# Pair 0 of an attention kernel: two vertical taps moved between two statistics, a copy and a store moved ahead, and one tile's additions moved from TensorE to VectorE

## The reference

```python
def _L0_conv_ref(x, W_qkv, W_proj, b_proj):
    qkv = x_flat @ W_qkv.T
    q, k, v = (qkv[0], qkv[1], qkv[2])
    var_v = jnp.var(v, axis=-1, ddof=1, keepdims=True)
    var_k = jnp.var(k, axis=-1, ddof=1, keepdims=True)
    scores = var_v @ jnp.swapaxes(var_k, -2, -1) * scale
    attn = jax.nn.softmax(scores, axis=-1)
    out = attn @ v
    out = out @ W_proj.T + b_proj
...
# layer 1, offset is fixed per group of 16 channels
    kern = jnp.exp(-(kx * kx + ky * ky) / (2.0 * SIGMA * SIGMA))
    kern = kern / kern.sum(axis=(1, 2), keepdims=True)
    out = lax.conv_general_dilated(shifted, kern_c[:, None, :, :], ..., feature_group_count=C)
...
x = x + _L0_conv_ref(_gn(x), L0_conv_W_qkv, L0_conv_W_proj, L0_conv_b_proj)
x = x + _L1_conv_ref(_gn(x), L1_conv_offset)
```

## Time and profile before

| | |
|---|---|
| median of three runs | 2025.69 us |
| the profiled execution | 2027.71 us |
| its span, first to last instruction | 2026.0 us |
| DVE busy | 1739.5 us (86%) |
| ACT busy | 1206.9 us (60%) |
| POOL busy | 276.1 us (14%) |
| mean granted TensorE clock | 0.997 of 2.4 GHz |

### The profile page before, as it was taken

One profiled execution on the slowest core, in us unless ns is written; L12 is line 12 of the kernel. 1 busy time (PEld: TensorE's weight loads), 2 busy tenths in 40 slices (PEclk: granted clock), 3 DMA queues, 4 the chain that ended last, 5 costly groups with the idle time before them and its releaser, 6 DMA issues.

```text
span 2026.0 us, 33485 instructions
## 1 busy us (share of the span) xinstructions
PE 1966.9 (97%) x12672; PEld 1109.0 (55%) x12672; DVE 1739.5 (86%) x3663; ACT 1206.9 (60%) x1322; POOL 276.1 (14%) x324
## 2 busy tenths in 40 slices
PE   5999989999999999999999999999999999999997
PEld 4755437563565536654375634756356553665443
DVE  7887686998779987899869998699878998599977
ACT  3667634776367762778527783477636776277820
POOL 2100001111012110111001111111101211011121
PEclk9999999999999999999999999999999999999999
DMA  8212313545235552356424562354523554134515
GB/s 331 84 54 64 105 63 87 138 141 169 85 116 158 148 177 63 116 137 185 139 64 128 152 190 86 92 139 137 167 84 118 155 154 129 43 116 137 157 42 187
DMA packets 110193, 255.19 MB, mean 126 GB/s; under 512 B 47312, under 2 KB 48080, under 8 KB 110032
## 3 DMA queue, kind: packets, MB, share of 16 engines
q0 software_dynamic: 31968, 116.41, 19.6%
q1 hardware_dynamic: 72016, 114.62, 18.7%
q10 hardware_dynamic: 6048, 22.02, 3.3%
HBM read 172.93 MB, written 79.73 MB: 125 GB/s over the span
## 4 chain that ended last, share of the span: by engine, by line
PE 60%; DVE 22%; issue 8%; DMA 5%; ACT 4%; SPq 0%; ACTq 0%; POOL 0%; DVEq 0%; POOLq 0%
PE ps L1405 23%; PE ps L1464 17%; PE ps L1447 16%; DVE bt L940 9%; DVE st L892 4%; ACT ring L714 3%; DMA a_sb<-a_rows 2%; PE ps L1422 2%; DMA a_rows<-at 2%; DVE bt L1064 1%; DVE bt L1061 1%; DVE xv L1074 1%; DVE xv L1077 1%; DVE xv L969 1%; DMA xv<-in_L_conv_W_qkv 1%
## 5 line engine op out<-in xcount | busy, mean ns | idle before, releaser
L714 ACT ACTIVATE ring<-a_sb,coef 128x1024 f32<-128x1024 f32 x768 | 817.9, 1137 | 22.9 <-issue 10.0
L1405 PE MATMUL ps<-wkv_hi,h_sp 128*128 128x256 f16 x4608 | 771.8, 273 | 12.0 <-DVE wkv_lo L1260 10.7
L1447 PE MATMUL ps<-ring,xv 128*64 128x512 f32 x3072 | 688.3, 596 | 7.5 <-ACT ring L714 6.2
L1405 PE MATMUL ps<-wkv_lo,h_sp 128*128 128x256 f16 x2304 | 628.9, 273 | 0.0
L940 DVE TENSOR_TENSOR bt<-bt,ring 128x1024 f32<-128x1024 f32 x528 | 615.3, 1214 | 3.0 <-ACT ring L714 1.9
L1405 PEld LDWEIGHTS ps<-wkv_hi,h_sp 128*128 128x128 f16 x4608 | 451.6, 98 | 91.7 <-issue 26.8
L1447 PEld LDWEIGHTS ps<-ring,xv 128*64 128x64 f32 x3072 | 209.2, 137 | 424.7 <-issue 384.1
L698 ACT ACTIVATE xv<-ps 128x256 f32<-128x256 f32 x192 | 72.6, 382 | 522.9 <-DVE st L892 522.0
L1464 PE MATMUL ps<-xv,wp_hi 128*128 128x512 f16 x1152 | 351.4, 380 | 6.2 <-DVE xv L1184 4.5
L892 DVE BATCH_NORM_STATS2 st<-ps 128x6 f32<-128x64 f32 x1536 | 218.0, 214 | 116.1 <-PE ps L1405 115.1
L1405 PEld LDWEIGHTS ps<-wkv_lo,h_sp 128*128 128x128 f16 x2304 | 225.8, 98 | 26.7
(11 more groups left out here) (174 smaller groups left out, 1349.8 us busy)
## 6 DMA issues: line engine op xcount, KB each, us to landing
a_sb<-a_rows SPq DMA_DIRECT2D x96, 512.0 KB, 4.5
out<-xv POOLq DMA_DIRECT2D x84, 512.0 KB, 5.3
xv<-in_x POOLq DMA_DIRECT2D x48, 512.0 KB, 3.6
h_sp<-in_x ACTq DMA_DIRECT2D x42, 512.0 KB, 5.1
shift_rows<-bt POOLq DMA_DIRECT2D x42, 512.0 KB, 3.4
bt<-r_rows SPq DMA_DIRECT2D x80, 256.0 KB, 4.2
bt<-in_x SPq DMA_DIRECT2D x24, 512.0 KB, 9.3
shift_rows<-ring SPq DMA_DIRECT2D x12, 528.0 KB, 15.5
```

The source lines that it names most:

```text
L714: nc.scalar.activation(ring_of(p, s, m), a_sb[:, h % 4, :], ACT.Exp, scale=coef[:, h, m:m + 1]).then_inc(s_exp, 1)
L1405: last = nc.tensor.matmul(ps[:, kv_bank[u % 2], half * 2 * P:(half + 1) * 2 * P], h_sp[:, k, hp, m * P:(m + 1) * P], wkv[wpart][:, k, q * ...
L1447: last = nc.tensor.matmul(ps[s * HD:(s + 1) * HD, o_bank[p % 2] + j, :], v_sb[:, p, m, s * HD:(s + 1) * HD], ring_of(p, s, m)[:, j * HALF: ...
```

## The change

Four edits:

1. `MD[0]` goes from 7 to 8. In pair 0 of each of the eight images DVE adds key tile 7 as well, and PE's sum over that tile's exponentials is left out.
2. Where a layer 1 runs beside (seven images), `taps_y` of tile 0 goes from behind the additions of key tile 3 to between the statistics of unit 6 and those of unit 7.
3. `middle_tap` of tile 0 goes on ACT from behind the exponentials of key tile 3 to behind those of key tile 0.
4. The residual store of tile 0 goes on POOL from behind the first reduction of the next image (`k_reduce`) to ahead of the square root of layer 1's group statistics (`group_pow`, L444).

```diff
-        MD = (7, 8, 8, 8, 6, 8)
+        MD = (8, 8, 8, 8, 6, 8)
...
+            def store_residual(b, t):
+                pool.wait_ge(s_x1, (b + 1) * PU)
+                hold(pool, s_held_pool)
+                pool.dma_start(out_t[b, :, t, :], x1[:, t, :]).then_inc(s_res, 16)
+
             def layer1(b, with_next):
                 for t in range(CT + 1):
                     if t < CT:
                         k_reduce(b + 1, t)
-                        pool.wait_ge(s_x1, (b + 1) * PU)
-                        hold(pool, s_held_pool)
-                        pool.dma_start(out_t[b, :, t, :], x1[:, t, :]).then_inc(s_res, 16)
+                        if t:
+                            store_residual(b, t)
...
             def body(b, with_next):
+                store_residual(b, 0)
                 group_pow(pool, "y", b)
                 layer1(b, with_next)
...
                         exps(b, p, m)
                         if p and m == 2:
                             d_copy(b, p - 1, later)
+                        if later and m == (3 if p else 0):
+                            middle_tap(l1, p)
                         if m == 3:
-                            if later:
-                                middle_tap(l1, p)
...
                     if p == 0:
                         kv_stats(b, nxt)
+                        if later:
+                            taps_y(l1, 0, g_t, t_t)
                         kv_stats(b, nxt + 1)
                         variances(b, 1)
...
                             if later:
-                                taps_y(l1, p, g_t, t_t)
+                                if p:
+                                    taps_y(l1, p, g_t, t_t)
```

## The result

The changed kernel takes 2049.6 us in the median of 4 runs (2048.44 to 2051.94), the kernel before 2026.2 us beside it: 1.0115 times as long, with a 95% interval of 1.0103 to 1.0128. It is slower by 23 us. The forecast was 2045.7 us with a range of 2028 to 2056; the time lies inside, 3.9 us above the forecast. The profiled execution took 2048.44 us, with a span of 2046.4 us against 2026.0 before, so the two traces differ by 20.4 us.

The account below looks back on a forecast made before the run. PE, busy for 97% of the span, was taken to bound the kernel. Seven images at 6.8 - 3.9 us (+20.3) and image 0 (-0.3) on 2027.7 gave 2047.7; less 2.0 for the median, 2045.7 us, range 2028 to 2056.

Parts of the forecast that it names:

- W - 3.9 us per image: Pair 0 with a layer 1 beside: change in one image's time, by DVE's path, never better than -0.88 us.
- W: Time from the issue of g_t's store to the issue of the window load; 9.3 us in image 2 before, forecast 6.8.
- gaps of 1.7 us and 1.4 us on PE: PE's expected idle times in pair 0: some 1.7 us before key tile 1, some 1.4 us at the pair's end.
- The nearest row: Image 4 before, where g_t's store was issued after the residual store's packets, together with the two broadcasts: W of 7.3 us.
- The upper end, 9.3: Highest W considered, in us: the store-to-load time stays as it was in image 2 before.
- Nothing gives this back later.: Claim that PE's new gaps in pair 0 are not recovered, since PE has no idle time elsewhere; largest wait sums to 6.2 us.
- my sum: Forecast for the profiled execution: +20.3 us for seven images, -0.3 for image 0, on 2027.7, giving 2047.7 us.
- The rival by the rule on queues: DMA engines alternate between g_t's store and the first broadcast packet by packet: W 4.9, +6.7 us, about 2032 us; no separate chance.
- The clock rival: PE's gaps also lower its clock, 3.2 us of work lost once in each of seven images: +22 us, 2068 us; chance 0.04.

Follow-up runs that it names:

- e4: The changed kernel with MD[0] back at 7 and the y taps back behind key tile 3, keeping only the middle tap and residual store moves; 2055.1 us.
- e5: The changed kernel with the two broadcasts for pair 0 of images 1 to 7 writing 16 of 128 partitions; 2026.8 us.
- e7: The changed kernel with g_t made earlier in phase A, so that its store is issued before the broadcasts; 2026.1 us.
- e3: The changed kernel with the residual store of tile 0 back in its old place; 2052.5 us.
- e2: The kernel before with MD[0] = 8 alone and no move; 2043.9 us.
- e8: The kernel before with the residual store of tile 0 moved and nothing else; 2028.0 us.
- e1: The changed kernel with all three moves kept and MD[0] back at 7; 2052.6 us.
- e10: The kernel before with MD[0] = 8 and 16 more matmul records, their sums discarded, put into PE's gap at pair 0's end; 2036.8 us.

## Why the prediction was right, and where it was off

**The mechanism.** Right at each place that it named. In image 2 ACT was idle for 4.99 us ahead of the tap (about 4 forecast), the y taps waited for ACT's row, unit 7's statistics had no gap ahead of them, and PE had new waits at two places. e4 shows ACT's path to be enough for the loss, e5 that the broadcasts' traffic is its source.

**The formula, W - 3.9 us per image.** Its sum over the seven measured values of W is 7 x (7.48 - 3.9) = 25.1 us, and the pairs grew by 25.1. That it holds to a tenth is partly luck: single images lie up to 0.8 us above it (image 4: 2.7 by the formula, 3.5 measured) and 0.3 us below it. It rests on DVE ending last, with gaps of 1.7 us and 1.4 us on PE. Measured in image 2: 2.21 us and 0.19. The first is longer with W. The second is shorter because ACT's path had a term that I left out: the halved clock stretched the three key tiles by 7.07 - 6.09 = 0.98 us. That used up most of the slack before DVE's end, so what ends last is the same in most images. In image 3 it is not: the gap was 3.57 us, PE ran at 0.50 from the gap's end at 824.8 to 830 us and had no wait for DVE, and the pair grew by 5.6 us for 5.2 by the formula.

**W.** Forecast 6.8, measured 7.48: the term that was mis-sized, worth 7 x 0.68 = 4.8 us. The step that failed is the correction from 7.3 us, W of image 4 before, down to 6.8, because the broadcasts would be 0.7 us further along when the store is issued. In image 4 before, the store was issued 0.05 us *ahead* of the first broadcast. In the changed kernel the first broadcast goes 0.4 to 0.7 us ahead of it in images 1, 2, 3, 6 and 7 (in image 2 at 564.33 against 565.02), and there W is 7.69 to 9.07: longer, not shorter. It was under 7.3 where the broadcasts went 1.6 us ahead (image 4, 6.58) and where the store went ahead by 0.6 us (image 5, 5.48). The nearest row would have been the better choice without the correction. The upper end, 9.3, was image 2's alone, where the mean before was 8.53. From the residual store I expected no more than a small share of W, and the 0.7 us above bear that out.

**"Nothing gives this back later."** Wrong: of the 25.1 us 20.4 arrive. Image 0's pair gives 0.3 as forecast, and the start of the trace 1.4, which is no work of the change. The remaining 3 us are small waits of PE that went away. Between 300 and 1940 us its waits sum to 12.1 us before and 26.6 after; without the six gaps ahead of key tile 1 (15.3) and those on DVE's additions at the end of pair 0 (2.1), 9.2 us are left of them, 2.9 us less. I read PE's waits as too small to matter, 6.2 us in the largest row; some of them are gone when PE arrives later at the following pairs, which is my reading and was not tested. This and the too small W nearly cancel in the traces, 20.4 against 20.0, and that is luck.

**The median.** The profiled execution's 2048.4 us is 0.7 from the 2047.7 of my sum. The rest of the 3.9 us is that I took 2.0 us off, the distance of the profiled execution from the median in the kernel before; after, the median lies 1.2 us *above* the profiled one. That correction was noise.

**The rival by the rule on queues.** In its section on queues, rings and completion order the Trainium skill (DMA: Bandwidth & Descriptors) has the engines take turns packet by packet, which gave W = 4.9 us and 2032. With the broadcasts issued 0.7 us ahead of the store, W is 7.69. In three windows that follow each other from 564.9 to 570.0 us, SP's queue (q1) moved 0.08, 0.25 and 0.71 MB, which is all of the two broadcasts. POOL's (q0) moved nothing in the first two, and this in the third, from 567.4 to 570.0 us (packets, MB, share):

```profile
q1 hardware_dynamic: 200, 0.71, 66.9%
q0 software_dynamic: 21, 0.09, 8.0%
```

With even turns from its issue on, the store's 0.5 MB would have gone with the first 0.5 MB of the broadcasts. Its packets begin more than 4 us after the issue here (none from 565.02 to 569.3 us), and 0.8 to 1.8 us after it in e7's image 2, so the time that the rule gives does not come, and the measurement decides. Turns as such are seen: in image 5, from 1298.5 to 1299.5 us, q1 moved 0.25 MB and q0 0.19 MB. Why the store's packets begin late behind the broadcasts is open. Image 5 and e7 show the other order: issued first, the store is through in 4.0 to 5.5 us.

**The clock rival.** I gave it 0.04, since "the gaps I expect are half as long". It happened: behind each of the six gaps of 2.2 to 3.6 us ahead of key tile 1 the clock was 0.50. It did not add 22 us: its price on PE was 0.98 us in five of the six images and 7.99 - 6.09 = 1.90 us in image 3, where I had 3.2 for each, and in this kernel most of that fell into slack before DVE's end, as e3's two images show. In e2, where the gap stands at the pair's end and nothing is behind it to absorb, it cost about 7 us in all.

## What to carry to other kernels

Before a consumer is moved to an earlier place on an in-order engine, look in the trace for when its data lands, not for how much idle time the new place has: here the gap was wide enough for the work, and the data came 5 us late. When the data comes by DMA, look at what else is in the engines at its issue: here that decided, and putting the small urgent store ahead of the large one (e7) was worth more than taking traffic away elsewhere (e8). Price a new gap of 2 us or more on PE with about 1 us beyond its length (none to 1.9 us here), and ask whether anything ends later and hides it.

## What the runs showed of the hardware

- Behind PE gaps of 2.2 us (the changed kernel) and 2.5 us (e2) the granted clock was 0.50 for about 3 us, and in image 2 of the changed kernel three key tiles took 7.07 us where they take 6.09 at full clock. It did not fall behind every such gap: it stayed at 1.00 behind gaps of 2.05 and 2.51 us in e1, 2.28 to 2.71 us in three images of e4, 2.58 to 3.27 us in three images of e3. Behind e7's gap of 1.16 us at the pair's end it stayed at 1.00, as it did behind e10's of 0.65. The stretch behind e7's:

```profile
596.00:599.00 3.00, 3.00 (x28) 1.95 (x26) 2.96 (x3) 3.00 (x4) 0.09 (x1) 1.00 0.00 0
```
- The two row broadcasts from DRAM to 128 partitions do not move evenly in time. In the changed kernel SP's queue moved 0.26 MB from 566 to 568 us at a share of 31.9%, although no other queue moved anything, and 0.67 MB in the next 2 us at 81.7%. Why it is slow at first, and why the store's packets wait behind it, is open; no run was made for either.
- The order of issue of two transfers 0.6 us apart changes a wait by microseconds: the store of g_t had landed and the load was issued 7.7 to 9.4 us after it behind the broadcasts (0.7 us earlier, before and changed kernel), and 4.1 to 6.3 us after it where it went 0.6 to 1.0 us ahead of them (changed kernel, e2, e3, e10).
